# Memory tokens of a linear attention as a factor and a matrix formed once, in a fused attention and convolution kernel

## The reference, cut to what matters

```python
mk = jnp.broadcast_to(mem_kv[0][None], (b, HEADS, DHEAD, MEM))     # 4 memory tokens, the same for all samples
mv = jnp.broadcast_to(mem_kv[1][None], (b, HEADS, DHEAD, MEM))
k = jnp.concatenate([mk, k], axis=-1)
v = jnp.concatenate([mv, v], axis=-1)
q = jax.nn.softmax(q, axis=-2) * attn_scale
k = jax.nn.softmax(k, axis=-1)                                     # over the 1028 tokens, per channel
context = jnp.einsum('bhdn,bhen->bhde', k, v)
out = jnp.einsum('bhde,bhdn->bhen', context, q)
out = jnp.einsum('oc,bchw->bohw', w_out, out) + b_out[None, :, None, None]
```

## Time and profile before

| what | value |
|---|---|
| median of three runs | 440.95 us (440.26 to 441.42) |
| the profiled execution | span 438.3 us; the page gives no time of its own for it |
| TensorE busy, share of the span | 414.9 us, 95% |
| VectorE | 351.1 us, 80% |
| ScalarE | 296.2 us, 68% |
| GpSimd | 265.0 us, 60% |
| DMA queue of SP | 37.0% of 16 engines |

### The profile page before, as it was taken

The page is one execution under the profiler, slowest core; times in us unless marked ns, Lnnn a source line. Parts: engine busy times, 40 slices in busy tenths (PEclk is TensorE's granted clock), DMA queues, the critical chain, the costliest instruction groups (busy, mean ns, idle before and its releaser), DMA issues.

```text
span 438.3 us, 8984 instructions
## 1 busy us (share of the span) xinstructions
PE 414.9 (95%) x2651; PEld 367.2 (84%) x2651; DVE 351.1 (80%) x769; ACT 296.2 (68%) x908; POOL 265.0 (60%) x249
## 2 busy tenths in 40 slices
PE   7789898999999999999999999999999999999987
PEld 6688787979898988889797988888898989778777
DVE  3565989797989889797989798898989696987540
ACT  2785857868676858778676868688686868654131
POOL 4754739567583939486674939385874748252330
PEclk9999999999999999999999999999999999999999
DMA  7420242216252442506262433516162523424331
GB/s 195 178 98 2 96 193 98 120 72 241 99 218 119 146 192 95 229 28 228 98 241 96 175 160 126 208 53 230 52 239 96 192 97 114 175 98 191 146 143 48
DMA packets 19075, 61.63 MB, mean 141 GB/s; under 512 B 3024, under 2 KB 4320, under 8 KB 19040
## 3 DMA queue, kind: packets, MB, share of 16 engines
q1 hardware_dynamic: 19040, 61.21, 37.0%
HBM read 19.29 MB, written 8.39 MB: 63 GB/s over the span
## 4 chain that ended last, share of the span: by engine, by line
PE 43%; DVE 22%; issue 17%; ACT 11%; DMA 2%; POOL 1%; DVEq 0%; SPq 0%; ACTq 0%; POOLq 0%
PE ps_conv L1282 13%; PE ps_y L1214 6%; PE ps_att L1181 5%; DVE w_full L1020 5%; ACT expert_raw L662 4%; DVE y_scaled L908 3%; DVE route_terms L974 3%; ACT qk L601 3%; PE ps_y L1204 3%; PE ps_y L1220 3%; DVE q_exp L860 2%; DMA xa<-in_x_dram 2%; ACT squares L574 2%; PE ps_qkv L1160 2%; PE ps_qkv L1162 2%
## 5 line engine op out<-in xcount | busy, mean ns | idle before, releaser
L601 ACT ACTIVATE qk<-ps_qkv,scale 128x256 f32<-128x256 f32 x128 | 55.7, 471 | 5.9 <-PE ps_qkv L1162 3.5
L544 POOL TENSOR_TENSOR left_hi<-zeros 128x32 fp32r<-128x32 f32 x16 | 9.4, 585 | 78.9 <-DMA right_lo<-img_lo 78.9
L668 ACT ACTIVATE w_hi<-w_full 128x1152 fp32r<-128x1152 f32 x16 | 18.7, 1168 | 52.9 <-DVE w_full L1026 52.9
L537 POOL TENSOR_TENSOR w_lo<-w_full,w_hi 128x1152 fp32r<-128x1152 f32 x16 | 42.8, 2675 | 11.0 <-ACT w_hi L668 6.1
L492 POOL TENSOR_TENSOR x_lo<-x,x_hi 128x1024 fp32r<-128x1024 f32 x16 | 38.4, 2399 | 13.1 <-ACT x_hi L591 13.1
L518 POOL TENSOR_TENSOR scale<-ssq,minus_half 128x8 f32<-128x8 f32 x16 | 26.2, 1639 | 32.9 <-DVE ssq L901 32.9
L642 ACT ACTIVATE y_scaled<-ps_y 128x128 f32<-128x128 f32 x128 | 33.5, 294 | 14.5 <-PE ps_y L1214 14.5
L1160 PE MATMUL ps_qkv<-wqk_hi,x_hi 128*128 128x256 f32 x128 | 40.6, 317 | 2.5 <-ACT x_nt L582 1.3
L1282 PE MATMUL ps_conv<-left_lo,w_hi 128*128 128x512 f32 (+2 forms) x96 | 40.6, 424 | 0.0
L1282 PE MATMUL ps_conv<-img_hi,w_hi 128*128 128x512 f32 (+1 forms) x96 | 36.4, 393 | 2.5 <-issue 1.4
L1282 PE MATMUL ps_conv<-right_hi,w_hi 128*128 128x512 f32 (+2 forms) x96 | 37.9, 395 | 0.0
(11 more groups left out here) (172 smaller groups left out, 1337.5 us busy)
## 6 DMA issues: line engine op xcount, KB each, us to landing
xa<-in_x_dram SPq DMA_DIRECT2D x16, 512.0 KB, 4.1
xb<-in_x_dram SPq DMA_DIRECT2D x16, 512.0 KB, 4.7
left_hi<-img_hi SPq DMA_DIRECT2D x16, 511.5 KB, 2.9
right_hi<-img_hi SPq DMA_DIRECT2D x16, 511.5 KB, 3.7
left_lo<-img_lo SPq DMA_DIRECT2D x16, 511.5 KB, 2.9
right_lo<-img_lo SPq DMA_DIRECT2D x16, 511.5 KB, 3.7
out_dram<-expert_raw SPq DMA_DIRECT2D x15, 512.0 KB, 2.9
expert_raw<-_conv_expert_weight_dram SPq DMA_DIRECT2D x1, 1728.0 KB, 9.0
```

What stands on the lines that cost most here:

```text
L537: nc.gpsimd.tensor_tensor(w_lo[p][:, :, :].rearrange("p t o -> p (t o)"), w_full[:, :], w_hi[p][:, :, :].bitcast(F32).rearrange("p t o -> ...
L601: nc.scalar.activation(qk[:, t, :], ps_qkv[t % 2][:, 0:QK], ACT.Copy, scale=scale1[:, t:t + 1]).then_inc(qkv_done, 1)
```

## The change

With the maximum M of a channel over all 1028 tokens and m over its four memory keys, the memory keys' exponentials are exp(key - m), which is the same for all samples, times exp(m - M). So the memory part of the context is a matrix formed once, scaled per channel. The new kernel forms once: the weights exp(key - m) and their sum (mem_sum), the product with the memory values, masked to heads and multiplied by the output weights (mem_mix, 128 x 128). Per sample ScalarE forms the factor exp(m - M) and the denominator (the sum of the sample's exponentials plus mem_sum times the factor). GpSimd multiplies mem_mix by the factor and the inverted denominator (memory_share) and adds the bias share (mix_start). VectorE's evacuation of mix adds that in place of the bias share. The two memory products on TensorE, the subtraction on VectorE, the exponential on ScalarE and four memsets fall away. k_shift becomes a transposition. In TensorE's list two of the three convolution products behind y_transpose go ahead of it.

```diff
@@ GpSimd @@
+            def memory_share(b, p):
+                if not past(b, 1):
+                    pool.wait_ge(setup_dve, 7)
+                pool.wait_ge(mem_factor_done, b + 1)
+                if past(b, 1):
+                    pool.wait_ge(mix_base_done, b)
+                pool.wait_ge(k_rsum_done, b + 1).then_inc(mem_share_started, 1)
+                nc.gpsimd.tensor_scalar(mem_share[:, :], mem_mix[:, :], mem_factor[:, :], k_rsum[:, :], ALU.mult, ALU.mult).then_inc(mem_share_done, 1)
+
+            def mix_start(b, p):
+                pool.wait_ge(mem_share_done, b + 1)
+                if past(b, 1):
+                    pool.wait_ge(mix_done, b)
+                nc.gpsimd.tensor_tensor(mix_base[:, :], mem_share[:, :], bias_share[:, :], ALU.add).then_inc(mix_base_done, 1)
...
             def step(t, p):
                 do(rms1, t, p, 3)
+                do(memory_share, t, p, 4)
                 do(routing_products, t, p, 5)
+                do(mix_start, t, p, 4)
                 do(x_scale, t, p, 3)
@@ ScalarE @@
-            def memk_exponent(b, p):
-                act.wait_ge(memk_sub_done, b + 1)
-                nc.scalar.activation(memk_exp[0:MEM, :], memk_exp[0:MEM, :], ACT.Exp).then_inc(memk_exp_done, 1)
+            def memory_weights():
...
+                nc.scalar.activation(memk_weight[:, :], memk_rel[:, :], ACT.Exp, accum_out=mem_sum[:, :]).then_inc(setup_act, 1)
+
+            def memory_factor(b, p):
...
+                nc.scalar.activation(mem_factor[:, :], k_max_all[:, :], ACT.Exp, bias=memk_max[:, :], scale=-1.0).then_inc(mem_factor_done, 1)
+
+            def k_denominator(b, p):
...
+                nc.scalar.activation(k_den[:, :], mem_sum[:, :], ACT.Identity, bias=k_x[:, C:C + 1], scale=mem_factor[:, :]).then_inc(k_den_done, 1)
...
-                do(memk_exponent, t, p, 2)
+                do(memory_factor, t, p, 2)
                 do(k_exponent, t, p, 2)
...
                 do(k_x_evacuate, t, p, 2)
+                do(k_denominator, t, p, 2)
                 do(x_copy, t, p, 1, 1)
@@ VectorE @@
             def k_subtract(b, p):
                 dve.wait_ge(k_shift_ps, b + 1)
                 if past(b, 1):
-                    dve.wait_ge(context_ps, b)
-                v.tensor_tensor(memk_exp[0:MEM, :], memk_t[:, :], ps_att[0:MEM, 0:HID], ALU.subtract).then_inc(memk_sub_done, 1)
+                    dve.wait_ge(k_x_ps, b)
...
             def k_sums(b, p):
-                dve.wait_ge(k_x_done, b + 1)
+                dve.wait_ge(k_den_done, b + 1)
...
-                v.reciprocal(k_rsum[:, :], k_x[:, C:C + 1]).then_inc(k_rsum_done, 1)
+                v.reciprocal(k_rsum[:, :], k_den[:, :]).then_inc(k_rsum_done, 1)
...
                 dve.wait_ge(k_rsum_done, b + 1)
+                dve.wait_ge(mix_base_done, b + 1)
...
-                v.scalar_tensor_tensor(mix[p][:, :], ps_att[:, 0:C], k_rsum[:, :], bias_share[:, :], ALU.mult, ALU.add).then_inc(mix_done, 1)
+                v.scalar_tensor_tensor(mix[p][:, :], ps_att[:, 0:C], k_rsum[:, :], mix_base[:, :], ALU.mult, ALU.add).then_inc(mix_done, 1)
@@ TensorE, once, in step 1 @@
+            def memory_keys():
+                pe.wait_ge(setup_act, 2)
+                tr(ps_att[0:MEM, 256:384], memk_weight[:, :], ident[:, :]).then_inc(setup_pe, 1)
+            def memory_context():
+                pe.wait_ge(setup_dve, 5)
+                mm(ps_att[:, 384:512], memv_t[:, :], memk_t[:, :], start=True, stop=True).then_inc(setup_pe, 1)
+            def memory_mix():
+                pe.wait_ge(setup_dve, 6)
+                mm(ps_att[:, 128:256], mem_context[:, :], wout_t[:, :], start=True, stop=True).then_inc(setup_pe, 1)
@@ TensorE, every sample @@
-                mm(ps_att[:, 0:HID], k_max_all[:, :].to_broadcast((128, 128)), ident[:, :], start=True, stop=True).then_inc(k_shift_ps, 1)
+                tr(ps_att[:, 0:HID], k_max_all[:, :].to_broadcast((128, 128)), ident[:, :]).then_inc(k_shift_ps, 1)
...
-                pe.wait_ge(memk_exp_done, b + 1)
...
-                mm(ps_att[:, 0:CEXT], memk_exp[:, :], mem_ones[:, :], start=True, stop=False)
                 for t in range(NT):
-                    last = mm(ps_att[:, 0:CEXT], k_exp[:, t, :], x_nt[p][:, t, :], start=False, stop=(t == NT - 1))
+                    last = mm(ps_att[:, 0:CEXT], k_exp[:, t, :], x_nt[p][:, t, :], start=(t == 0), stop=(t == NT - 1))
...
-                mm(ps_att[:, 0:HID], memv_t[:, :], memk_exp[:, :], start=True, stop=False)
-                mm(ps_att[:, 0:HID], wqkv_t[:, QK:QKV], x_k[:, :], start=False, stop=True).then_inc(context_ps, 1)
+                mm(ps_att[:, 0:HID], wqkv_t[:, QK:QKV], x_k[:, :], start=True, stop=True).then_inc(context_ps, 1)
...
                 keep_busy(t, "y_transpose")
+                conv(2)
                 do(y_transpose, t, p, 2)
-                conv(3)
+                conv(1)
```

More of the change, by code:

```diff
@@ L93, in attention_condconv_kernel @@
         memk_max = sb("memk_max", [128, 1])
+        memk_rel = sb("memk_rel", [128, MEM])
+        memk_weight = sb("memk_weight", [128, MEM])
+        mem_sum = sb("mem_sum", [128, 1])
         memk_t = sb("memk_t", [MEM, HID])
-        memv_t = sb("memv_t", [128, HID])
-        mem_ones = sb("mem_ones", [128, CEXT])
+        memv_t = sb("memv_t", [MEM, HID])
+        mem_context = sb("mem_context", [128, HID])
+        mem_mix = sb("mem_mix", [128, C])
         expert_raw = sb("expert_raw", [128, K, C * TAPS])
@@ L131, in attention_condconv_kernel @@
         k_exp = sb("k_exp", [128, NT, HID])
-        memk_exp = sb("memk_exp", [128, HID])
+        mem_factor = sb("mem_factor", [128, 1])
+        k_den = sb("k_den", [128, 1])
+        mem_share = sb("mem_share", [128, C])
+        mix_base = sb("mix_base", [128, C])
         q_max = sb("q_max", [128, NT * HEADS])
@@ L236, in attention_condconv_kernel @@
         k_sub_done = sem("k_sub_done")
-        memk_sub_done = sem("memk_sub_done")
         k_exp_done = sem("k_exp_done")
-        memk_exp_done = sem("memk_exp_done")
+        mem_factor_done = sem("mem_factor_done")
+        k_den_done = sem("k_den_done")
+        mem_share_started = sem("mem_share_started")
+        mem_share_done = sem("mem_share_done")
+        mix_base_done = sem("mix_base_done")
         q_max_done = sem("q_max_done")
@@ L436, in _ @@
             nc.gpsimd.memset(zeros[:, :], 0.0)
[L437 to L440, removed]
             for p in range(2):
@@ L601, in qkv_evacuate @@
                 nc.scalar.activation(qk[:, t, :], ps_qkv[t % 2][:, 0:QK], ACT.Copy, scale=scale1[:, t:t + 1]).then_inc(qkv_done, 1)
-            def memk_exponent(b, p):
-                act.wait_ge(memk_sub_done, b + 1)
-                nc.scalar.activation(memk_exp[0:MEM, :], memk_exp[0:MEM, :], ACT.Exp).then_inc(memk_exp_done, 1)
+            def memory_weights():
+                act.wait_ge(setup_dve, 4)
+                nc.scalar.activation(memk_weight[:, :], memk_rel[:, :], ACT.Exp, accum_out=mem_sum[:, :]).then_inc(setup_act, 1)
+            def memory_factor(b, p):
+                act.wait_ge(k_max_all_done, b + 1)
+                if past(b, 1):
+                    act.wait_ge(mem_share_done, b)
+                    act.wait_ge(k_den_done, b)
+                nc.scalar.activation(mem_factor[:, :], k_max_all[:, :], ACT.Exp, bias=memk_max[:, :], scale=-1.0).then_inc(mem_factor_done, 1)
+            def k_denominator(b, p):
+                if not past(b, 1):
+                    act.wait_ge(setup_act, 2)
+                act.wait_ge(k_x_done, b + 1)
+                act.wait_ge(mem_factor_done, b + 1)
+                if past(b, 1):
+                    act.wait_ge(k_rsum_done, b)
+                nc.scalar.activation(k_den[:, :], mem_sum[:, :], ACT.Identity, bias=k_x[:, C:C + 1], scale=mem_factor[:, :]).then_inc(k_den_done, 1)
             def k_exponent(b, p):
@@ L618, in k_x_evacuate @@
                     act.wait_ge(x_k_ps, b)
-                    act.wait_ge(k_rsum_done, b)
+                    act.wait_ge(k_den_done, b)
                 nc.scalar.activation(k_x[:, :], ps_att[:, 0:CEXT], ACT.Copy).then_inc(k_x_done, 1)
@@ L716, in step @@
                 once(expert_evacuate, t, 2, 5)
+                once(memory_weights, t, 1)
                 do(k_x_evacuate, t, p, 2)
+                do(k_denominator, t, p, 2)
                 do(x_copy, t, p, 1, 1)
@@ L750, in constants @@
                 dve.wait_ge(setup_dve, 3)
+                v.tensor_scalar(memk_rel[:, :], mem_c[:, 0, :], memk_max[:, :], None, ALU.subtract).then_inc(setup_dve, 1)
+            def memory_keys():
+                dve.wait_ge(setup_pe, 3)
+                v.tensor_copy(memk_t[:, :], ps_att[0:MEM, 256:384]).then_inc(setup_dve, 1)
+            def memory_context():
+                dve.wait_ge(setup_pe, 4)
+                v.tensor_tensor(mem_context[:, :], ps_att[:, 384:512], head_mask[:, :], ALU.mult).then_inc(setup_dve, 1)
+            def memory_mix():
```

(6 more changed lines are left out.)

10 lines of the change are left out of this document (6 added, 4 removed).

## The result

The changed kernel takes 445.72 us (median of four runs, 444.82 to 446.02) where the kernel before took 441.06 beside it (four runs): the ratio is 1.0114, with a 95% interval of 1.009 to 1.0138. The change makes the kernel 4.7 us slower; 439.0 was forecast, and the range ended at 442.8. The profiled span grew from 438.3 to 443.1 us, by 4.8.

A forecast was written before the change was run, and what follows sets the result against it. The prediction took a TensorE-VectorE loop as the bound, with GpSimd's rstd then delaying the routing. Ordinary steps 1.3 us, late steps -0.15, ends 1.0, set-up -0.2: 1.95 us off 440.95 gave 439.0 us, range 433.0 to 442.8.

The forecast's parts named there:

- The step that failed: GpSimd behind rstd: x1 is needed only by the next step's transposition; rstd itself was to move by 0.48 us.
- the prediction's two stretches: Each period: y transposition to routing on TensorE, 11.22 us; routing to next y_scaled, where no gain was counted.
- TensorE's removals: Memory products dropped from key contexts and contexts: 0.37 us gained at the key contexts, 0.59 us with the contexts.
- The moved products: Two convolution products ahead of the y transposition: 0.44 us off the path, filling TensorE's wait at no cost.
- The two additions: GpSimd's new memory_share and mix_start ahead of rstd: 0.32 and 0.47 us long, bounds up to 0.63 each.
- The routing waits for rstd: In ordinary steps the routing product starts 0.14 us after GpSimd's rstd, at 347.97 instead of 348.16: 0.19 us gained.
- Late steps: Three of twelve steady steps, with GpSimd's zero columns at 2.09 us: each 0.05 us slower, 0.15 us together.
- Start and tail: Ends of the kernel, where GpSimd has less to do: 1.0 us gained, less 0.2 us for set-up.
- TensorE was not the bound: Rival that TensorE bounds and GpSimd keeps up: 0.59 us gained per step, 433.2 us; chance 0.17.
- zero columns: Rival that GpSimd's zero columns, held by VectorE's two-tensor operations, become late in every step: 444.7 us; chance 0.13.
- VectorE's waits for xa: Rival that the xa transfer ends last in most steps, so only the ends gain: 440.2 us; chance 0.20.
- Theory H: From the experiments: VectorE instructions reading two SBUF tensors are held until the GpSimd instruction beside them ends; with one in PSUM, not.

The follow-up runs named there:

- The shortened x1: The changed kernel with GpSimd's x1 made for only the first 512 of its 1024 columns: 441.79 us, ratio 1.0017.
- the pair left out: The changed kernel without its two GpSimd instructions, memory_share and mix_start, so without the memory tokens' share of the mix: 437.79 us, ratio 0.9914.
- the version of 439.65 us: The changed kernel with the memory tokens added by VectorE instead of GpSimd, the sum written into PSUM before mix: 439.65 us, ratio 0.9962.

## Why the prediction was wrong

**The step that failed** is "Behind rstd GpSimd has x1, needed only by next step's transposition", and with it the stretch of VectorE taken as unchanged. x1's result is indeed not needed, but its place in time is: VectorE's route_terms reads two tensors in SBUF, and begun beside x1 it ended only 0.27 us behind x1. The margin was 349.26 - 349.06 = 0.20 us, and the forecast itself moved rstd by 0.48. Its own numbers gave the collision: with rstd ending at 347.83, x1 (0.51 us behind rstd, 1.20 long) ends at 349.54; with the routing at 347.97, route_terms (1.10 behind it) begins at 349.07. Where the routing waits for rstd, x1 always follows it at the same distance, so the collision comes in every such step. Nor does later slack take it up: in the step shown GpSimd runs from w_lo's start at 338.98 to rstd's end at 351.66 with no gap over 0.12 us, and w_lo waits for the filters that the gates make, so late gates come back as a late rstd. That loop through GpSimd is not among the prediction's two stretches. The shortened x1 shows the price, some 4 us, 2.6 of them the holds themselves.

The terms one by one:

- *TensorE's removals*: 0.37 us at the key contexts was forecast and 0.36 measured. The further 0.22 from the contexts did not reach outputs, which started 349.74 - 340.67 = 9.07 us behind the transposition of y against 9.44: mix waited for mix_base. "outputs start by 345.8, no later than above" was wrong by 0.2 us, counted from the transposition; mix_base ended 8.47 us behind the transposition, as forecast (8.41), but 0.60 us passed from there to outputs.
- *The moved products*: no cost, as forecast, and no gain of their own (445.14 us with the order back).
- *The two additions*: mix_start 0.456 us, forecast 0.47; memory_share 0.477, forecast 0.32, inside its bounds of 0.15 to 0.63. Line 485 scaled to 128 columns was too low by 0.16.
- *The routing waits for rstd*: right, and with 0.15 us from rstd's end to the product, taken as 0.14. The gain of 0.19 became 11.22 less 351.81 - 340.67 = 11.14, so 0.08 us; the difference is of the size of memory_share's error.
- *Late steps*: 0.05 us each was forecast. In the kernel before, the late routings of the eleven periods are the fourth, eighth and twelfth, 11.67, 11.70 and 11.50 us behind y_scaled; in the kernel after they are the fourth, fifth and fourteenth, 11.85, 12.05 and 11.69: 0.72 us more together. Only the fourth is late in both, and it lost 0.18.
- *Start and tail*: 1.0 us of gain less 0.2 was forecast, 0.39 + 0.49 us of loss measured. How much of the start is the change's stays open: the first y_scaled ended at 45.38 us with the pair left out and all the set-up there, at 45.36 before, and at up to 47.59 in other kernels of this study.

**The rivals.** None had the mechanism. TensorE was not the bound: from the third to the fourteenth, every routing product started 0.14 or 0.15 us behind the end of rstd. One of the four zero columns took over 1.8 us in three of the sixteen steps, in four in the kernel before; they became late in other steps, not in all. VectorE's waits for xa fell from 11.3 to 8.3 us in sum. The rule quoted for the zero columns was the right rule at the wrong place. The Trainium skill (SBUF — State Buffer, SBUF: two separate sides) puts it more sharply: VectorE with two SBUF inputs and a GpSimd instruction that reads SBUF take the shared ports in turn, whole instructions at a time, and the loser waits. The trace agrees in route_terms, in spread beside route_prod and in mix, by the ends given above. It does not agree beside GpSimd's power, where no hold is seen (last section).

## What to carry to other kernels

Before instructions are put on GpSimd, write down for each stretch that they push what VectorE runs beside it, and whether that has two tensors in SBUF (x1, x_nt and route_prod held such instructions here, the power did not); the margin to the next such instruction is a resource like a wait, even where nobody needs GpSimd's result. An instruction that has to run beside a busy GpSimd is safer with one tensor in PSUM, even if the sum must be written there for it. A gain on the busiest engine is worth only what the chain behind it lets through: here 0.36 us measured and 0.22 forecast, 0.58 us a step, were freed on TensorE, and the version of 439.65 us kept 0.09 of them (its eleven periods last 370.97 - 105.21 = 265.76 us, 24.16 each, against 24.25).

## What was not expected of the hardware

- A hold costs by the end of the other instruction, not by its share: two spreads of one column took 0.81 us beside route_prod and 0.37 without it, and a mix of 128 columns that read two tensors in SBUF 1.21 us beside x_nt, 0.35 where one of them was in PSUM. What is left behind the other's end goes with the columns: 0.27 to 0.28 us for 257 (route_terms), 0.15 to 0.16 for 128 (mix), 0.02 for one (spread).
- The turn can go either way. In the step of 347 of the kernel after, the second spread ran beside mem_share (347.66 to 348.13) and both spreads were done in 0.37 us, by 347.95. In the step of 151 they took 0.47 and ended with mem_share, at 152.00. GpSimd:

```profile
151.51 0.49 POOL L527 TENSOR_SCALAR mem_share<-mem_mix,mem_factor,k_rsum 128x128 f32<-128x128 f32 x1
```

VectorE:

```profile
151.53 0.47 DVE L845 SCALAR_TENSOR_TENSOR spread<-dev,meanvar 128x1 f32<-128x1 f32 x2
```

What decides the turn was not tried.

- Theory H is too wide for every GpSimd instruction. Beside the power that follows x1 (scale), VectorE's img_lo, with two tensors in SBUF, was not held. In the kernel before it took 1.27 to 1.29 us in the fifteen steps in which it began 0.6 us behind the power, and 1.28 in the one in which it ran alone. GpSimd, then VectorE:

```profile
350.83 1.64 POOL L518 TENSOR_TENSOR scale<-ssq,minus_half 128x8 f32<-128x8 f32 x1 [1.77 <-DVE ssq L901]
...
351.44 1.27 DVE L956 SCALAR_TENSOR_TENSOR img_lo<-x,nmean,img_hi 128x1024 fp32r<-128x1024 f32 x1
...
416.89 1.28 DVE L956 SCALAR_TENSOR_TENSOR img_lo<-x,nmean,img_hi 128x1024 fp32r<-128x1024 f32 x1
```

- Where the routing product had to wait for rstd, its two passes took 0.67 us instead of 0.60, and route_y began 0.70 us behind their start instead of 0.64.
